# Transposes and copies of the next norm's first three quarters placed ahead of the layer border, and a new order of VectorE's work with sums on GpSimd in L3Attention

## What is computed

```python
x = x + _L0_xattn_ref(_layernorm(x, axis=-1), ctx_1024, ...)   # 16 heads, 257 context rows per sequence
x = x + _L0_attn_ref(_layernorm(x, axis=-1), ...)
x = x + _L0_ffn_ref(_layernorm(x, axis=-1), ...)
...
x = x + _L3_attn_ref(_layernorm(x, axis=-1), ...)
x = x + _L3_ffn_ref(_layernorm(x, axis=-1), ...)               # a GRU over the sequence, then experts
```

```python
attn = jax.nn.softmax(scores, axis=-1)                 # dense, 16 heads; then ctx, dense_output
aw = jax.nn.softmax(QK, axis=-1)
topv, topi = jax.lax.top_k(aw, kk)                     # kk = 6 of 32
sparse_attn = zeros.at[bi, si, topi].set(topv); sparse_attn /= sum + 1e-9
fused = sig * dense_output + (1.0 - sig) * sparse_output
x = _layernorm(src + fused, ln1_g, ln1_b)
ff = jax.nn.relu(x @ ff1_w.T + ff1_b) @ ff2_w.T + ff2_b
return _layernorm(x + ff, ln2_g, ln2_b)
```

## Time and profile before

| | us |
|---|---|
| median of 3 runs | 2988.69 |
| lowest, highest | 2987.17, 2990.55 |
| the profiled execution | 2988.34 |
| its span in the trace | 2986.6 |
| its mean granted TensorE clock, share of full | 0.958 |

### The profile page before, as it was taken

One profiled execution on the slowest core, in us unless ns is written; L12 is line 12 of the kernel. 1 busy time (PEld: TensorE's weight loads), 2 busy tenths in 40 slices (PEclk: granted clock), 3 DMA queues, 4 the chain that ended last, 5 costly groups with the idle time before them and its releaser, 6 DMA issues.

```text
span 2986.6 us, 69018 instructions
## 1 busy us (share of the span) xinstructions
PE 2773.4 (93%) x26509; PEld 1781.9 (60%) x26509; DVE 1757.0 (59%) x5682; ACT 1308.3 (44%) x3510; POOL 706.8 (24%) x1552
## 2 busy tenths in 40 slices
PE   8999998997999979998699987699999999999898
PEld 7888885565577756665467755444444444444465
DVE  6787777766478867559568867712232232232544
ACT  4665565552288842358368864311121121111221
POOL 2444441000178830034037751000000000000000
PEclk9999999999999989869889999889999999999999
DMA  5111110000021100410021130030000000000000
GB/s 134 50 48 46 48 41 8 3 3 6 20 55 49 43 25 1 118 60 2 6 58 41 41 133 27 15 126 1 1 1 1 1 1 1 1 1 1 1 1 15
DMA packets 125903, 92.03 MB, mean 31 GB/s; under 512 B 41283, under 2 KB 122566, under 8 KB 124230
## 3 DMA queue, kind: packets, MB, share of 16 engines
q1 hardware_dynamic: 125574, 87.61, 10.3%
HBM read 83.89 MB, written 3.67 MB: 29 GB/s over the span
## 4 chain that ended last, share of the span: by engine, by line
PE 78%; DVE 10%; issue 5%; DVEq 3%; ACT 2%; POOLq 1%; POOL 1%; DMA 0%; SPq 0%; ACTq 0%
PE banks L3558 25%; PE banks L491 3%; PE banks L926 3%; PE banks L897 2%; PE banks L910 2%; PE banks L935 2%; PE banks L3981 2%; PE banks L3972 2%; PE banks L521 2%; PE banks L3970 2%; PE banks L500 2%; PE banks L471 2%; PE banks L508 2%; PE banks L509 2%; PE banks L1759 1%
## 5 line engine op out<-in xcount | busy, mean ns | idle before, releaser
L1011 ACT ACTIVATE probs<-probs,nbias 128x257 f32<-128x257 f32 x512 | 254.3, 501 | 0.0
L1227 POOL TENSOR_SCALAR probs<-probs,rinv 128x257 f32<-128x257 f32 x512 | 237.6, 483 | 25.0 <-DVE rinv L1109 21.8
L3558 PE MATMUL banks<-Wz,hT 128*64 128x256 f32 x2048 | 226.4, 379 | 0.0
L3831 POOL COPY rb<-hT 128x512 f32<-128x512 f32 x32 | 35.8, 1118 | 801.7 <-ACT hT L3634 777.4
L3558 PE MATMUL banks<-Wn,hT 128*64 128x512 f32 x1024 | 225.4, 593 | 0.0
L3558 PE MATMUL banks<-Wr,hT 128*64 128x512 f32 x1024 | 225.2, 592 | 0.0
L3558 PEld LDWEIGHTS banks<-Wz,hT 128*64 128x64 f32 x2048 | 147.0, 137 | 87.7 <-issue 18.3
L3800 DVE TENSOR_TENSOR pr<-hb,banks 128x512 f32<-128x512 f32 x32 | 22.0, 688 | 298.4 <-PE banks L3613 298.4
L717 POOL TENSOR_SCALAR probs<-probs,rinv 128x257 f32<-128x257 f32 x256 | 120.1, 482 | 205.0 <-DVE rinv L657 204.4
L3558 PEld LDWEIGHTS banks<-Wr,hT 128*64 128x64 f32 x1024 | 73.5, 137 | 132.6 <-issue 128.0
L3558 PEld LDWEIGHTS banks<-Wn,hT 128*64 128x64 f32 x1024 | 70.9, 137 | 129.5 <-issue 129.5
(11 more groups left out here) (664 smaller groups left out, 6485.0 us busy)
## 6 DMA issues: line engine op xcount, KB each, us to landing
kvT<-in_ctx_T SPq DMA_DIRECT2D x192, 128.5 KB
kv<-in_ctx SPq DMA_DIRECT2D x64, 128.0 KB
kv<-in_ctx SPq DMA_DIRECT2D x32, 256.0 KB
W<-in_L_ffn_W_T SPq DMA_DIRECT2D x2, 2048.0 KB
Wr<-in_L_ffn_w_hh_T SPq DMA_DIRECT2D x1, 4096.0 KB
Wn<-in_L_ffn_w_hh_T SPq DMA_DIRECT2D x1, 4096.0 KB
Wz<-in_L_ffn_w_hh_T SPq DMA_DIRECT2D x1, 4096.0 KB
v_last<-v_last SPq DMA_DIRECT2D x192, 8.0 KB, 1.6
```

The source lines that it names most:

```text
L1011: i = e.activation(s, s, ACT.Exp, bias=self.nbias[v][:, r:r + 1], scale=self.scale, accum_out=self.rows_sum[v][:, r:r + 1])
L1227: e.tensor_scalar(s, s, self.rinv[v][:, r:r + 1], 1.0, ALU.mult, ALU.mult)
L3558: mm = e.matmul(self.bank[b][hf * BATCH:(hf + 1) * BATCH, 0:n], lhs, rhs, start=start, stop=stop, tile_position=(0, hf * BATCH))
```

## The change

Each stage gets three methods, `pe_early`, `act_early` and `pool_early`, called ahead of the wait on `closed`. By default they hold the transposes and copies of quarters 0 to 2; they are empty for the first stage and L1Attention, so this applies to ten of the eleven borders. The banks of three stages are renamed to ones that the stage before no longer uses. The memsets of `of_row` move to `pool_early`, and its place in SBUF to the part that is free ahead of the border. In L3Attention all four dense softmaxes of a round stand ahead of the sparse part, `scale_rows` with both gains and the sum into X move to GpSimd with three new signals, and the last quarter of X is added by a new function on VectorE that does not make the normalised rows first.

```diff
+    def pe_early(self, e):
+        self.norm_pe(e, (0, 1, 2))
+
+    def act_early(self, e):
+        self.norm_act_yT(e, (0, 1, 2))
...
@@ HeadCrossAttention, L0Attention, L3Attention
+    TURN_BANKS = (0, 1, 7, 3)
+    TURN_BANKS = (1, 2, 3, 6)
-    TURN_BANKS = (4, 5, 6, 0)
+    TURN_BANKS = (0, 1, 5, 6)
@@ L2CrossAttention.act (the same in L1Ffn, L2Attention, L2Ffn, L3Ffn)
         e.activation(self.warm[:, :], self.prog.ones[:, 0:1], ACT.Sqrt)
-        self.norm_act_yT(e, (0, 1))
         self.norm_act_std(e)
-        self.norm_act_yT(e, (2, 3))
+        self.norm_act_yT(e, (3,))
@@ L3Attention.dve
-        e.tensor_tensor(self.be1[:, :], self.be1[:, :], self.b_f2[:, :], ALU.add)
-        e.drain()
         for r in range(N + 1):
             m = r - 1
             if m >= 0:
                 self.norm.start_dve(e, self.s1)
+                self.x1_added.wait_ge(e, m - 1)
                 self.norm.rows_dve(e, self.s1, self.s2[m % 2])
                 e.drain().then_inc(self.s2_normed.up(), 1)
             if r < N:
                 self.add_values(e, r)
                 self.sparse_max(e, r)
-                attn.softmax_dve(e, 4 * r)
-                attn.softmax_dve(e, 4 * r + 1)
-            if m >= 0:
-                self.x1_turned.wait_ge(e, m + 1)
-                self.scale_rows(e, m, self.g1, self.be1)
+                for s in range(4):
+                    attn.softmax_dve(e, 4 * r + s)
+                self.sparse_top(e, r)
+                self.sparse_rest(e, r)
             if m >= 1:
-                self.add_x(e, m - 1)
+                self.x1_added.wait_ge(e, m)
+                self.next_statistics(e, m - 1)
             if r == N:
                 for q in range(3):
                     self.next_rows(e, q)
-            if r < N:
-                self.sparse_top(e, r)
-                attn.softmax_dve(e, 4 * r + 2)
-                attn.softmax_dve(e, 4 * r + 3)
-                self.sparse_rest(e, r)
             if m >= 0:
                 s2 = self.s2[m % 2]
+                self.x1_scaled.wait_ge(e, m + 1)
                 self.w2_mm.wait_ge(e, m + 1)
...
-            if m >= 0:
+            if 0 <= m < N - 1:
                 self.norm.rows_dve(e, s2, s2)
-                e.drain()
+                e.drain().then_inc(self.x1_normed.up(), 1)
...
-        self.add_x(e, N - 1)
+        self.last_add(e, self.s2[(N - 1) % 2])
+
+    def last_add(self, e, s2):
+        norm, at = self.norm, lambda u: slice(u * P, (u + 1) * P)
+        x = self.prog.X[:, (self.ROUNDS - 1) * R4:self.ROUNDS * R4]
+        for u in range(4):
+            e.scalar_tensor_tensor(s2[:, at(u)], s2[:, at(u)], norm.mv[:, 2 * u:2 * u + 1], self.g2[:, :], ALU.subtract, ALU.mult)
+        norm.std.wait_ge(e, norm.var.count)
+        e.reciprocal(norm.rstd[:, :], norm.rstd[:, :])
+        self.x1_added.wait_ge(e, self.ROUNDS)
+        e.drain()
+        for u in range(4):
+            e.scalar_tensor_tensor(x[:, at(u)], s2[:, at(u)], norm.rstd[:, u:u + 1], x[:, at(u)], ALU.mult, ALU.add)
+        e.drain()
@@ L3Attention.pool, in the loop behind y_bo and behind the loop
+            if r:
+                self.scale_x1(e, r - 1)
+            if r > 1:
+                self.add_x(e, r - 2)
+        self.scale_x1(e, self.ROUNDS - 1)
+        self.add_x(e, self.ROUNDS - 2)
+        x = self.prog.X[:, (self.ROUNDS - 1) * R4:self.ROUNDS * R4].rearrange("p (t d) -> p t d", d=P)
+        e.tensor_tensor(x, x, row4(self.be2), ALU.add).then_inc(self.x1_added.up(), 1)
+
+    def scale_x1(self, e, m):
+        self.x1_turned.wait_ge(e, m + 1)
+        self.scale_rows(e, m, self.g1, self.be1).then_inc(self.x1_scaled.up(), 1)
@@ L3Ffn
-    def pool(self, e):
-        E = self.E
+    def pool_early(self, e):
         e.memset(self.of_row[:, :], 0.0)
@@ each engine's program
             for s in stages:
+                s.pe_early(e)
                 closed.wait_ge(e, 4 * s.index)
```

58 lines of the change are left out of this document (25 added, 33 removed).

## The result

| | before | after |
|---|---|---|
| median, us | 2989.62 (4 runs) | 2957.09 (4 runs) |
| lowest, highest | 2987.17, 2994.83 | 2952.54, 2959.48 |
| profiled execution, its span | 2988.34, 2986.6 | 2952.54, 2950.7 |
| mean granted TensorE clock in it | 0.958 | 0.965 |

The ratio is 0.9894, 95% interval 0.9877 to 0.9912: 32.5 us less, where 21.3 were forecast. Before has 66 runs in them with a mean of 2986.9 us (2974.99 to 2995.09), the changed kernel 15 in three with a mean of 2960.2 (2952.54 to 2973.40). That is 26.7 us (33.8, 22.8 and 28.4 in the means of the three comparisons), and each program's own runs are spread by some 5 us around their mean. So the first 32.5 were in part a good draw, and a single comparison of a few runs tells less than its interval says.

A forecast was written before the change was run, and what follows sets the result against it. TensorE, busy 93%, was taken to bound the kernel, leaving 213 us of waits to win. Borders 13.15, L3Attention's order 7.55 and GpSimd 0.6 sum to 21.3 us off 2988.7, giving 2967.4; range 2956 to 2981.

The forecast's parts named there:

- L3Attention: Border into L3Attention: early transposes and copy save 2.0 us, after which the fourth quarter bounds.
- likeliest case: Whole kernel at 2967.4 us, own range 2960 to 2975 with terms at half below; chance 0.52.
- L0Ffn: Border into L0Ffn: VectorE's 0.52 us wait for the copy goes after its weight unpacking; 0.4 us.
- L2Xattn: Border into L2Xattn: earlier root saves 2.35 us, less 0.5 for products longer at the slow clock; 1.85 us.
- L3Ffn: Border into L3Ffn: twelve transposes run within TensorE's 6.50 us wait and products start with the border; 2.6 us.
- L1Ffn: Border into L1Ffn: 1.53 us of transposes go, but a part stays for the fourth quarter's copy; 1.2 us.
- L3Xattn: Border into L3Xattn: all twelve transposes ahead of the keys go, less an overlap; 2.2 us.
- L2Ffn: Border into L2Ffn: the root frees 1.12 us of VectorE, which the next products wait for; 1.1 us.
- The first rival: Borders don't pay: TensorE stays longer at the slow clock, giving back 12.9 us, about 2980; chance 0.15.
- 7.55 and 0.6: In L3Attention: the new order saves 7.55 us over four rounds; GpSimd's sums and the last addition net 0.6.
- The tail: End of L3Attention: last addition saves 1.3 us, GpSimd's late `x1_added` costs about 0.7; net 0.6.
- The clock rival: Around the border into L2Attention: half-clock stretch of 47 us ends 20 us earlier, bringing 10 us, 2957; chance 0.10.

The follow-up runs named there:

- the halves: Two kernels: every border as changed with L3Attention as before, 2971.07 us; L3Attention as changed with every border as before, 2977.41 us.
- transposes_only: The changed kernel with ScalarE's early copies put back behind the border, TensorE's transposes still early; 2972.22 us, ratio to before 0.9944.
- after_again: The changed kernel run again without an edit; 2963.57 us, ratio to before 0.9918.
- root_first: Before, with ScalarE's fourth-quarter root ahead of the copies of the first three at six borders, transposes still late; 2990.13 us, ratio to before 1.0016.
- border_busy: Changed kernel plus 3 unread products ahead of the border into L3Ffn, and GpSimd's third-quarter sum ahead of the fourth's gain; 2954.45 us, ratio to before 0.9906.
- l11_only: Before, with L3Attention's new order, sums on GpSimd and last addition, every border as before; 2977.41 us, ratio to before 0.9967.

## Why the prediction was right

**The direction and the range** held. The kernel is faster by 26.7 us over all runs, by 32.5 in the first comparison; forecast were 21.3. The sum of terms was near what the halves gave, 14.6 and 8.3 against 13.15 and 8.15, and too small by 5 to 11 for the whole. A slip in it: terms at half would give 2978, not the 2975 that its likeliest case ends at.

**The borders.** The early transposes start in TensorE's waits at all ten. The sign that the prediction set, that they end before the border, held at three (L0Ffn, L2Xattn, L3Ffn); at L1Ffn and L3Xattn they ended with it, at the other five 0.3 to 1.6 us behind. The single terms were not so good. L3Xattn and L3Attention gave 2.8 and 3.2 where 2.2 and 2.0 were forecast. The copies are not the reason, since transposes_only has them late and lost 0.2 and nothing there. TensorE's clock is a part of it. The 15 us from the statistics at the border into L3Xattn, before and after (columns as in the earlier trace rows), and the first products with yT in L3Attention, before and in after_again:

```profile
1515.60:1530.60 15.00, 14.32 (x51) 9.42 (x52) 8.39 (x28) 4.59 (x13) 4.46 (x19) 0.54 0.49 118
...
1498.50:1513.50 15.00, 12.97 (x63) 7.83 (x62) 10.50 (x39) 5.93 (x17) 7.03 (x20) 0.89 0.48 124
...
1770.69 3.78 PE L2953 MATMUL banks<-yT,inT 128*128 128x512 f32 x4 [0.30 <-ACT yT L237]
...
1761.78 1.88 PE L2960 MATMUL banks<-yT,inT 128*128 128x512 f32 x4
```

In such a window at L3Xattn the five profiles with late transposes (root_first too) have 10.2 to 13.7 us at half clock, the eight with early transposes and copies 3.4 (transposes_only 6.8). The products of L3Attention took 3.08 to 3.78 us in those five and 1.88 to 1.98 in eight of nine with early transposes. That is no draw of one execution, and the forecast had no term for it. L0Ffn and L1Ffn gave nothing to speak of: VectorE's unpacking and the fourth quarter's rows bound. L2Xattn gave 1.0 of 1.85: the root did come free as the order showed, worth 2.3 us to the first product as forecast, but the products behind it ran at 5.09 us, at the slow clock; the 0.5 put on that was too little. L2Ffn's 0.9 against 1.1 is partly luck: the term was put on the root, and root_first, which frees the root alone, gained next to nothing there. L3Ffn gave 0.9 of 2.6 in the medians: "the products start with the border" was right, and they took 5.28 us, after TensorE had stood 3.7 us since the transposes. Where transposes came late they took 2.82 themselves, and the 24 entries behind them ran in 2.99 and 3.19 in two of four profiles, in 5.12 in the other two. Against these two, of which the profile that the prediction was made from is one, the gain is 2.45, near the term.

**The first rival, that the borders don't pay for the clock's sake,** was wrong as a whole, right at L2Xattn and, against half of the late profiles, at L3Ffn, and the wrong way round at L3Xattn and L3Attention. border_busy shows that its price at one of them, 2.4 us, can be had back.

**L3Attention.** The step that failed is the one that costed the order and GpSimd's part apart, 7.55 and 0.6. Alone they do not give that: 0.7 us each in the layer's time of one profile, 3.3 less and 1.7 more in its idle time, and by the ratios of the times 4.8 (0 to 9) and 1.2 (-3 to 5), the first of which reaches up to the whole. What stands in its place is one mechanism with two conditions, and its size as a pair, 8.3 by the times, met 8.15. By the pair's trace the rounds met their terms too: idle time from one round's first turn to the next's fell by 2.7 and 2.2 us for rounds 2 and 3 (8.4 to 5.7, 7.6 to 5.4, l11_only), where 2.5 and 2.3 were put. The text had the piece in hand, since it costed GpSimd's sums at nothing for the cover they have; it didn't ask what the cover was, which is the order. Round 1 gave nothing, where 0.45 was put. The tail gave 1.5 (from the last turn to the border 19.6 us before, 18.1 in l11_only), where 0.6 was put: the lateness of `x1_added` fell in TensorE's shadow. The prediction's sign of being wrong, idle time at the statistics of X, did come, with 8.03 us, and cost 0.5.

**The clock rival** was given 0.10 as a stretch ending 20 us earlier in L2Attention. The first profile had about that, 29 us of it instead of 47, and it brought 4.5 us (the offset to before rose from 10.0 to 14.5 in the layer), half of the 9 that 18 us would give at twice the speed. Its fault was to be treated as one event. Single layers draw their own stretches in each execution, as L2Attention did with 7 us, and the times of one program are spread by 5 us.

**What stays open.** Of 26.7 us in the mean, 15.4 to 18.1 are idle time. The other 9 to 11 are less busy time, at a mean granted clock of 0.962 against 0.9575 over the runs. (The idle part is itself uncertain by the 2 to 4 us of L2Attention.) That early transposes shorten slow stretches is shown at the borders into L3Xattn and L3Attention, by eight and nine profiles against five; into L0Ffn it is the other way (up to 3.2 us at half clock in the 15 behind the statistics, none with late transposes), and for the rest of the kernel nothing is shown. Why the clock is quicker at those two borders is not shown either.

## What to carry to other kernels

Split a profile's difference into idle and busy time of the bounding engine first: with the same instructions the busy part is the clock, and it may be half of what one comparison shows (20.5 of 35.9 us here). Cost an edit and the move that covers it as one term, and ask of each cover which edit makes it. Before a difference at half clock is called luck, look whether all profiles of one side have it: at one place here it was a draw, at two it was the kernel. Work moved forward into an engine's wait leaves a wait behind it: look at what runs first afterwards, and at which clock; a few products that nobody reads, in a wait that costs nothing, may be worth it, and in one that is too short they cost what they bring (each at one place here).

## What the runs showed of the hardware that was not expected

One layer with TensorE busy in all of 20 us stayed at half clock through them (after_again, 1305 to 1325), and the same instructions in another execution had left it 15 us earlier. The granted clock of a whole run ranged from 0.952 to 0.963 over 66 runs of one program, and its time with it (correlation -0.80). Behind four added products of 128x512, 6.08 us long, the same stretch was over, in the one profile that has them; another of 7 us followed 10 us later. The gain of 2.4 us that three such products bring at the border into L3Ffn was the same in both kernels that have them.
